# Graph network on one core: who rounds the source index, and when the matrix stores are issued

## The reference, cut to what matters

```python
edge_index = jnp.stack([src, dst])
x = _layernorm(x + _L0_gnn_ref(x, edge_index, W1, b1, W2, b2, Wres, bres))        # segment_sum(x[src], dst)
x = _layernorm(x + _L1_gnn_ref(x, src, dst, ...))     # two rounds, sum divided by the in-degree
x = _layernorm(x + _L2_gnn_ref(x, edge_index, edge_weight, W, bias, W_phi))       # four rounds, weighted sum
x = _layernorm(x + _L3_gnn_ref(x, edge_index_t, edge_attr_6, W, b, We, be))       # sum and edge attributes
```

## Time and profile before

| | us |
|---|---|
| median of 3 runs | 1131.49 (1131.43 to 1131.75) |
| the profiled execution, its time | 1133.12 |
| its span, first to last instruction | 1131.3 |
| PE / DVE / ACT busy in the span | 1030.5 / 528.0 / 284.9 |
| setup, until DVE's first one-hot (L698) | 65.79 |
| build, until ACT's last copy of pair 12 | from there to 283.6 |

### The profile page before, as it was taken

How to read it: one execution, slowest core, us unless ns; L and a number is a source line. 1 busy time by engine, 2 the same in 40 slices (tenths; PEclk the granted TensorE clock), 3 DMA queues, 4 the chain that set the end, 5 groups by cost and what they waited for, 6 DMA issues and landing times.

```text
span 1131.3 us, 25112 instructions
## 1 busy us (share of the span) xinstructions
PE 1030.5 (91%) x10553; PEld 627.2 (55%) x10553; DVE 528.0 (47%) x956; ACT 284.9 (25%) x588; POOL 54.1 (5%) x69
## 2 busy tenths in 40 slices
PE   1348898888899999999999999999999999999997
PEld 0247677667655655545556445574445744457455
DVE  6989898885633355422233222322222324344333
ACT  0467888888610000000000000000000001112100
POOL 4600000000000000000000000000000000000000
PEclk9657999999999999999999999999999999999999
DMA  8216677667995865877659877498765987655931
GB/s 247 72 3 257 273 321 303 277 279 329 358 412 220 324 221 223 342 288 282 252 177 413 321 277 275 147 408 323 312 239 194 360 348 289 256 185 212 412 129 32
DMA packets 55527, 299.56 MB, mean 265 GB/s; under 512 B 6880, under 2 KB 10354, under 8 KB 52019
## 3 DMA queue, kind: packets, MB, share of 16 engines
q1 hardware_dynamic: 49968, 288.14, 66.0%
q0 software_dynamic: 3344, 9.67, 2.6%
q10 hardware_dynamic: 2160, 0.98, 0.4%
HBM read 235.93 MB, written 62.86 MB: 264 GB/s over the span
## 4 chain that ended last, share of the span: by engine, by line
PE 75%; DMA 15%; DVE 5%; issue 2%; ACT 2%; SPq 0%; POOL 0%; ACTq 0%; DVEq 0%
PE ps L1307 46%; PE ps L1300 18%; DMA weight_mats<-arena 13%; PE ps L1262 4%; PE ps L1217 2%; PE ps L1275 2%; PE ps L1390 1%; PE ps L1414 1%; DMA arena<-edge_table,ptr 1%; ACT arena L1052 1%; DVE arena L700 1%; PE ps L1244 0%; DMA edge_table<-arena 0%; DVE arena L704 0%; DMA arena<-in_edge_w 0%
## 5 line engine op out<-in xcount | busy, mean ns | idle before, releaser
L1307 PE MATMUL ps<-arena 125*128 125x500 f32 (+2 forms) x700 | 267.5, 537 | 0.0
L1307 PE MATMUL ps<-arena,parts_even 125*128 125x500 f32 (+2 forms) x700 | 267.5, 537 | 0.0
L1307 PEld LDWEIGHTS ps<-arena,parts_even 125*128 125x128 f32 x700 | 129.4, 188 | 120.6 <-issue 106.7
L1307 PEld LDWEIGHTS ps<-arena 125*128 125x128 f32 x700 | 129.3, 188 | 120.6 <-issue 106.7
L1036 ACT ACTIVATE XT<-ps 128x500 f32<-128x500 f32 (+2 forms) x49 | 26.5, 540 | 492.0 <-PE ps L1275 492.0
L1300 PE MATMUL ps<-arena 125*128 125x500 f16 (+3 forms) x700 | 140.5, 354 | 1.7 <-DVE arena L737 1.3
L1414 PE MATMUL ps<-arena 64*128 64x52 f16 (+1 forms) x6500 | 105.1, 181 | 38.8 <-ACT arena L1052 20.4
L1050 ACT ACTIVATE arena<-ps 128x400 f16<-128x400 f32 (+1 forms) x195 | 125.7, 645 | 36.2 <-SPq L432 20.1
L1414 PEld LDWEIGHTS ps<-arena 64*128 64x128 f16 x6500 | 94.8, 96 | 57.5 <-ACT arena L1052 37.2
L1052 ACT ACTIVATE arena<-ps 128x400 f32<-128x400 f32 (+1 forms) x195 | 118.8, 609 | 0.0
L700 DVE TENSOR_TENSOR arena<-arena 128x5376 f16<-128x5376 f16 (+1 forms) x39 | 114.2, 2929 | 0.0
(11 more groups left out here) (187 smaller groups left out, 704.0 us busy)
## 6 DMA issues: line engine op xcount, KB each, us to landing
arena<-weight_mats SPq DMA_DIRECT2D x20, 3250.0 KB, 11.6
arena<-weight_mats SPq DMA_DIRECT2D x20, 3000.0 KB, 10.7
arena<-count_mats SPq DMA_DIRECT2D x15, 3125.0 KB, 14.6
weight_mats<-arena SPq DMA_DIRECT2D x12, 3125.0 KB, 14.9
count_mats<-arena SPq DMA_DIRECT2D x12, 1562.5 KB, 6.1
arena<-weight_mats SPq DMA_DIRECT2D x4, 2437.5 KB, 8.8
arena<-weight_mats SPq DMA_DIRECT2D x4, 2250.0 KB, 8.6
arena<-count_mats SPq DMA_DIRECT2D x3, 2343.8 KB, 9.6
```

The lines of the kernel that those rows point to most:

```text
L1307: ins = t.matmul(o, xs[:, k, :], rhs, start=(k == 0), stop=(k == NC - 1))
```

## The change

- ACT computes `hi`. A new `record_hi(i)` on ACT waits for `sd_in[i]` itself, and makes `hi32` and `hi` with two activations (bias from `magic_col`); DVE's `records(i)` loses L623 and L625 and waits for `rec_hi_ok` ahead of `lo32`. For the rounding both node numbers are stored in the table less `MID` = 12: DVE's L576 is a TENSOR_SCALAR instead of a cast, and the comparison uses the new `dmid`. POOL makes `dmid` and `magic_col` at its start (an iota and two memsets).
- The order in `records(i)` is another: counts, weights, both degree sums, then the wait, `lo32`, the lower part of the weight, `lo`; `rec_ok` is given by an instruction of its own after `lo`.
- The flags are gathered inside `records(5)`, behind its first two instructions; PE sums them ahead of the last eight `record_rows`; DVE copies `mode` ahead of the degrees.
- `W8_rep` (L668) and PE's product for it move ahead of `records(4)`.
- The lower part of x (L642) moves from between `records(2)` and `records(3)` to behind the one-hots of pair 0. PE waits for it behind pair 0.
- The roots (L1021) move to behind ACT's pair 0.
- SP stores a pair's counts and weights together once the weights are out, and goes on without waiting. The landings count in `mats_out[0]` and `mats_out[1]` (even and odd pairs), on which ACT waits itself. `load(0)` waits for both.

```diff
@@ SP, fast_loads @@
-                with sp.Fori(0, PAIRS - 1) as q:
-                    sp.wait_ge(counts_out, UNITS * q + UNITS)
-                    sp.dma_start(count_mats[bass.ds(q, 1)]...).then_inc(mats_out, 16)
-                    sp.wait_ge(weights_out, UNITS * q + UNITS + OUT_PAD)
-                    sp.dma_start(weight_mats[bass.ds(q, 1)]...).then_inc(mats_out, 16)
-                    sp.wait_ge(mats_out, 32 * q + 32)
-                    sp.sem_inc(stg_free, 1)
+                with sp.Fori(0, PAIRS // 2) as h:
+                    for odd in range(2):
+                        sp.wait_ge(weights_out, 2 * UNITS * h + UNITS * (odd + 1) + OUT_PAD)
+                        sp.dma_start(two_counts[bass.ds(h, 1), odd]...).then_inc(mats_out[odd], 16)
+                        sp.dma_start(two_weights[bass.ds(h, 1), odd]...).then_inc(mats_out[odd], 16)
...
                 sp.wait_ge(agg0_done, last + 2)
+                sp.wait_ge(mats_out[0], 32 * (PAIRS // 2) + MATS_PAD)
+                sp.wait_ge(mats_out[1], 32 * (PAIRS // 2) + MATS_PAD)
                 load(0)
@@ DVE @@
-            v.tensor_copy(t_rows[:, :, 0:2], t_pairs)
+            v.tensor_scalar(t_rows[:, :, 0:2], t_pairs, -float(MID), None, ALU.add)
...
-                v.tensor_tensor(cnt, sdw[0:NP, cs, :, 1], d_c[:, cs].to_broadcast([NP, n, SLOTS]), ALU.is_equal)
-                link(v.tensor_scalar(hi32[:, 0:n, :], source, 1.0 / NC, -0.5 + 0.5 / NC, ALU.mult, ALU.add))
+                link(v.tensor_tensor(cnt, sdw[0:NP, cs, :, 1], d_c[:, cs].to_broadcast([NP, n, SLOTS]), ALU.is_equal))
                 v.tensor_tensor(wm, weight, cnt, ALU.mult)
-                link(v.tensor_scalar(hi, hi32[:, 0:n, :], ROUND_MAGIC, -ROUND_MAGIC, ALU.add, ALU.add))
+                if i == RECS - 1:
+                    link(v.tensor_reduce(flags[0:NP, 1:2], cntR[:, 0:NC, last], AX, ALU.max))
+                    v.tensor_reduce(flags[:, 0:1], flags[:, :], AX, ALU.max).then_inc(flag_ok, 1)
+                link(v.tensor_reduce(S8[:, cs, 0], cnt, AX, ALU.add))
                 v.tensor_copy(w1, wm[:, :, 0:last])
+                v.tensor_reduce(S8[:, cs, 1], wm, AX, ALU.add)
+                dve.wait_ge(rec_hi_ok, i + 1)
                 link(v.scalar_tensor_tensor(lo32[:, 0:n, :], hi, -float(NC), source, ALU.mult, ALU.add))
...
+                v.tensor_tensor(w2, wm[:, :, 0:last], w1, ALU.subtract)
+                link(v.scalar_tensor_tensor(lo, lo32[:, 0:n, :], float(MID + 1), cnt[:, :, 0:last], ALU.add, ALU.mult))
+                dve.sem_inc(rec_ok, 1)
...
                 for u in range(STEPS):
                     produce(0, u)
+                lower_x()
@@ ACT @@
+            def record_hi(i):
+
+                cs, n = slice(REC_AT[i], REC_AT[i + 1]), REC_AT[i + 1] - REC_AT[i]
+                whole = hi32[i % 2][:, 0:n, :]
+                act.wait_ge(sd_in[i], 16 * n)
+                s.activation(whole, sdw[0:NP, cs, 0:SLOTS - 1, 0], ACT.Identity, bias=magic_col[0:NP, 0:1],
+                             scale=1.0 / NC).then_inc(rec_hi_chain, 1)
+                act.wait_ge(rec_hi_chain, i + 1)
+                s.activation(hiR[:, cs, 0:SLOTS - 1], whole, ACT.Identity, bias=magic_col[0:NP, 1:2]).then_inc(rec_hi_ok, 1)
+
+            record_hi(0)
+            record_hi(1)
...
-                    act.wait_ge(stg_free, q + 1)
+                    if first:
+                        act.wait_ge(mats_out[odd], MATS_PAD)
+                    else:
+                        act.wait_ge(mats_out[odd], 16 * q + (0 if odd else MATS_PAD))
...
                 pair(0, 0, first=True)
+                roots()
```

More of the change, by code:

```diff
@@ L79 @@
 ROUND_MAGIC = 1.5 * 2 ** 23
+MID = NC // 2
 def chunks_of(g):
@@ L313, in build_program @@
         weights_out = sem("weights_out")
-        stg_free = sem("stg_free")
-        mats_out = sem("mats_out")
+        mats_out = [sem(f"mats_out{i}") for i in range(2)]
         agg0_done = sem("agg0_done")
@@ L359, in build_program @@
         OUT_PAD = 4
+        MATS_PAD = 16
         def by_mode(eng, fast, general):
@@ L416, in fast_loads @@
             def fast_loads():
-                sp.sem_inc(stg_free, 2)
+                for i in range(2):
+                    sp.sem_inc(mats_out[i], MATS_PAD)
                 sp.wait_ge(deg_ok, 1)
@@ L660, in _ @@
             v.scalar_tensor_tensor(WT["L2_W"][:, :], ident[:, :], -GAMMA, WT["L2_W"][:, :], ALU.mult, ALU.add)
+            dve.wait_ge(w8_ps, 1)
+            v.tensor_copy(W8_rep[:, :], ps[:, SUM_BANK, 0:D]).then_inc(w8_ok, 1)
             records(4)
@@ L666, in _ @@
                             ps[0:NP, 5, 2 * D:4 * D].rearrange("p (i f) -> p i f", f=D), ALU.add).then_inc(wt_ok, 1)
-            dve.wait_ge(w8_ps, 1)
-            v.tensor_copy(W8_rep[:, :], ps[:, SUM_BANK, 0:D]).then_inc(w8_ok, 1)
             records(5)
-            link(v.tensor_reduce(flags[0:NP, 1:2], cntR[:, 0:NC, last], AX, ALU.max))
-            v.tensor_reduce(flags[:, 0:1], flags[:, :], AX, ALU.max).then_inc(flag_ok, 1)
             def degrees():
@@ L988, in _ @@
                 s.activation(XT[:, NP * GROUP_AT[g]:NP * GROUP_AT[g] + n], ps[:, 6 + g % 2, 0:n], ACT.Copy).then_inc(xt0_ok, 1)
+            record_hi(2)
             act.wait_ge(x_in, 32)
@@ L1005, in record_columns @@
                 ins.then_inc(col_ok, 1)
+            record_hi(3)
             for b in range(4):
@@ L1012, in _ @@
                     s.activation(WT[k][:, :], ps[:, 4, i * D:i * D + D], ACT.Copy).then_inc(wt_copied, 1)
+            record_hi(4)
             for b in range(4, 8):
                 record_columns(b)
+            record_hi(5)
             act.wait_ge(fold_ps, 1)
@@ L1019, in _, with roots @@
                 record_columns(b)
-            act.wait_ge(deg_ok, 1)
-            s.activation(degr[:, :], degr[:, :], ACT.Sqrt).then_inc(sq_ok, 1)
+            def roots():
+                act.wait_ge(deg_ok, 1)
+                s.activation(degr[:, :], degr[:, :], ACT.Sqrt).then_inc(sq_ok, 1)
             def relu_bias(q):
```

59 lines of the change are left out of this document (33 added, 26 removed).

## The result

The changed kernel takes **1120.93 us** (median of 4 runs, 1119.69 to 1121.46), the kernel before 1131.46 beside it: a ratio of 0.9899, interval 0.988 to 0.9918, or 10.5 us less. The forecast was 1115.2 in a range of 1107 to 1122. Direction and range held, but a third of the forecast gain did not come. The profiled execution took 1121.46 us with a span of 1119.7, against 1133.12 and 1131.3 before: the two traces are 11.6 us apart, 1.1 us more than the medians, because the profiled execution before was a slow one of its kernel.

What follows compares the result with a forecast made beforehand. The prediction took weight stores to set the build's pace, with DVE the path in the setup. An earlier pair 1 (4.3 us) plus faster pairs (12.0 us) made 16.3 us, from 1131.49 to 1115.2, range 1107 to 1122.

Steps and rivals of the forecast that it cites:

- (a): Records in the setup: taking L623 and L625, twelve instructions, off DVE gives 4.2 us.
- (c): Flags and mode, between last record and first one-hot: 1.1 us gained; 2.16 us before L698 taken for the branch, staying.
- (d): ACT's new record_hi work, 1.1 us each: DVE newly waits about 1.0 us (0 to 2) for the folded weights.
- (e): Last gather in the setup: with L642 gone it lands 2.6 us earlier and nobody waits; otherwise 0.9 us lost.
- (g): Pairs 0 and 1: pair 1 starts 4.3 us earlier (2.5 to 5.2), its own length kept the same.
- Rival 2: More gain: waits nearly vanish, pace 14.1 us, or pair 1 loses its 2.96 us stall; 1106 to 1110; chance 0.15.
- (h): Stores, pairs 1 to 11: two-pair cycle 30.1 us, a pair 15.06 instead of 16.26, 12.0 us gained.
- s: In the store cycle, time for SP to see a written pair and issue its store: 0.3 us, bounds 0 to 0.57.
- C: In the store cycle, ACT's time to write a pair: taken as 14.1 us, seen before as 13.74 and 14.86.
- 1: Pair stores: the slow DMA engine bounds them at 15.6 us apart; 6.6 us gained, 1120.6; chance 0.12.
- 3: SP's store issue is held by a full queue: pace stays 16.26 us, only the setup counts, 1127.2; chance 0.06.
- 4: Overlapping stores share engines and land later: pace 17.45 us, 7.6 us slower, 1139; evidence an 18.6 us landing; chance 0.04.

Runs made afterwards that it cites:

- e3: Changed kernel with PE giving the start value on sums_ok ahead of the flag product, not after its wait for ACT's twelfth column block; 0.9908 of the kernel before.
- e11: The kernel before, unchanged, run once more for its trace on another chip; ratio 0.9988.
- e2: The kernel before with only the new SP store loop and ACT's waits on mats_out; 0.9925 of the kernel before.
- e10: Changed kernel with pair 0's store held until PE is through pair 1; 0.9944 of the kernel before.
- e6: Changed kernel with five unused matmuls of 512 columns in each pair, where PE would idle; 0.9904 of the kernel before.
- e9: Changed kernel with early start value, lower x before the branch, fold copies before the last record_hi, five unused matmuls a pair; 1113.49 us, 0.9831 of the kernel before.

## Why the prediction was right, and where it was not

- **(a), (f) records and table**: right. ACT's pair of activations took 1.0 to 1.4 us (forecast 1.1) and fitted its idle time; L576's successor takes 1.01 us as the cast did. That the last record ended at 54.67 for 54.9 has some luck in it, since the first began 0.8 us early.
- **(b)** 3.41 us left the setup and stand behind pair 0 (73.41 to 76.82), as forecast.
- **(c) failed.** The idle 2.16 us in front of L698 were taken for the branch, because the columns that L698 waits for were done. The row named an ACT column block, and a second semaphore of the same instruction, PE's start value, hung on the twelfth block. So the length from the last record to the first one-hot was set by PE and ACT (4.4 us before, 4.7 now), and taking the flags out of DVE's part of it could gain nothing: the forecast 1.1 us went into a longer wait, 3.76 us. First one-hot 59.38 for 58.0: 1.4 us lost. e3 shows 2.8 us of the wait removable.
- **(d)** right: 0.81 us for 1.0.
- **(e)** right: with L642 gone from beside the gathers, none takes more than 1.14 us, where one took 3.55. In e11 and e2, where this instruction still stands there, the gather took 3.56 and 3.23 us, each time until 0.8 us after that instruction's end. By the rule of the Trainium skill, "SBUF — State Buffer", Who interferes with whom, that a VectorE instruction with two inputs in on-chip memory contends with a GpSimd instruction that reads there, this is what should happen. The traces agree. The TENSOR_REDUCE over x (L637, 3.49 us), which has one input, leaves the gathers beside it at 0.95 us in both kernels.
- **(g) mis-sized.** Pair 1's counts came 2.05 us earlier, forecast 4.3: 1.4 by (c), 0.6 by the longer stall (3.59 for 2.96, which is within the 2.6 to 4.5 of all traces), 0.25 of small shares. The prediction kept the stall without a reason, and that was luck. Rival 2 tied it to the first store, which e10 confirms, but expected the change to part the two; the new order issues the store ahead of pair 1 as the old one did.
- **(h) right in kind, one term mis-sized.** Issue to free buffer 15.85 (15.7), s 0.17 (0.3), but C 15.0 instead of 14.1, in four cycles of five. The prediction had both values of C in front of it, 13.74 after a wait of 1.85 and 14.86 after 2.52, with the clock of 0.50 beside the second, and chose near the first since the new waits are about 2 us. But the clock decides between them and not the wait alone: waits of 1.87 to 2.16 gave 15.0 to 15.15 us with s in four cycles with a fall, and 13.91 in the one without. The pace gave 9.0 us instead of 12.0; its lower bound was 8.3. Where the clock stayed up, the forecast cycle of 30.1 us measured 29.93 (e6, e9) and 30.04 (the changed kernel behind 182.51). (With C = 13.74 the formula gives 13.9 us and not 13.7.)
- **The sum**: 16.3 less 2.25 (g) less 3.0 (h) is 11.1, and `load(0)` moved by 11.16. The medians moved by 10.5.
- **Rivals.** 1 is out: e9's stores follow each other at 14.96 us, below its 15.6. 2's pace is out; only its remark on the stall held. 3 is out by the alternating issues, 4 by landings of 15.4 us at most. Its one piece of evidence was misread: the 18.6 us are not store 0's. Store 0's weights landed 14.2 us after their issue, and the 18.6 are those of the last pair, half as large and issued among the first loads. The weight stores of the kernel before, from 80 to 280 us and from 280 to 300:

```profile
DMA to landing us min/median/max: 14.2/14.9/15.0
```

```profile
DMA to landing us min/median/max: 18.6/18.6/18.6
```

## What to carry to other kernels

When a bracket names an engine that was long done, look for every semaphore that the waiting instruction needs and who gives it behind what; of 3.76 us of idle time taken for a branch, 2.8 were an increment standing behind a wait. When a wait is taken off a loop, ask which waits are left and how long they leave TensorE idle, because a wait that costs 2 us may cost another one by the clock; some unused matmuls in the gap are worth trying. Work moved to a queue inherits whatever stands ahead of it there, also on a chip where that comes late. And before a largest or smallest value of a view is given to one transfer, ask for a window with that transfer alone.

## What the runs showed that I had not expected

- A cycle lost 0.6 to 1 us to the clock after PE had idled 1.13 to 1.48 us: granted 0.50 for 3.41 us in 26 of 35 cases, for at least as long in all 20 with 1.80 to 1.90 us, and in none where the idle time was under 1 us. What spares the other nine is open.
- Adding five matmuls a pair (1.24 us of PE in e9's timeline) shortened a pair from 15.35 to 14.97 us, half of 30.70 and 29.93.
- A pair's stores (1562.5 and 3125 KB) issued before or during a loop's first pass were followed, 5.8 to 7.8 us later, by 2.6 to 4.5 us in which PE did nothing; it went on 1.2 to 1.6 us after a 16 KB packet of the `instruction` queue. With no store it idled 0.89 us there.
- On two of three chips PE waited 2 to 10 us at a time between the transposes of x in the setup, mostly with no releaser, and whole executions scattered by 4 to 14 us.
